# The opening of a two-layer graph transformer kernel, written out by hand: biases placed by matmuls, W1 split on VectorE, scores of group 1 ahead of the first PV, W2 loaded in two parts

## The chip, the cores and the metric

The kernel runs on one core of one Trainium2 chip. The metric is the device time in microseconds (us), lower is better. Below, TensorE is PE in the rows, VectorE is DVE, ScalarE is ACT, GpSimd is POOL and SyncE, which issues the DMAs, is SP.

## The reference

Input x is 128 graphs of 64 nodes with 384 features, adj is 128 x 64 x 64. Everything is fp32. Two layers follow each other.

```python
# layer 0: 8 heads of 48, feed-forward 384 -> 1536 -> 384
q, k, v = x @ wq + bq, x @ wk + bk, x @ wv + bv
attn = softmax(q @ k.T * 48**-0.5 + adj)
x1 = alpha1 * rms(x + (attn @ v) @ wo + bo) + gamma1
z  = alpha2 * rms(x1 + silu(x1 @ w1 + b1) @ w2 + b2) + gamma2
x  = layernorm(x + z)
# layer 1: 12 heads of 32, weights transposed, adj added twice (spatial and edge)
x  = layernorm(x + attention(x, 2 * adj) @ Wo.T + bo)
```

## The kernel before, in words

The 8192 nodes are cut into 32 groups of 256 (two tiles of 128, each of two graphs). Layer 0 goes through all groups, then layer 1; this case is about the opening of layer 0. Every fp32 matrix product is made of three passes over a high and a low part (`mm3`, L421): each operand is rounded on ACT ("high") and the rest is formed on DVE by a subtraction ("low"). So each weight and each activation is converted once on ACT and once on DVE before TensorE can read it.

Layer 0 is a software pipeline over steps g. In step g TensorE does, in this written order, `pv` of group g-1 (probabilities times v), `scores` of g, the feed-forward of g-2 (`ffn1` and `ffn2` in six blocks, with `attn_out` of g-1 in its middle), and `qk` and `values` of g+1. In the steps 0 to 2 `qk` and `values` of g+1 stand ahead of the feed-forward instead (`ahead`). Each engine has its own list in program order and waits on semaphores; nothing reorders at run time. SP's list is the only one that issues DMAs, so a load that waits holds back every load and store behind it.

Between the matrix products there are three round trips through DRAM, which turn a tile of rows into a tile of columns: DVE transposes 32x32 blocks, SP stores them in eight DMAs, waits for them, and loads the turned tile in one DMA; ACT and DVE make its high and low part. The round trips are p (`turn_p` L873, `store_p` L245, `load_pt` L252, `take_pt` L650), the context (`turn_ctx` L889, `store_ctx` L261, `load_ctxt` L265, `ctxt_high` L658), and x1 (`turn_x1` L912, `store_x1` L269, `load_x1t` L273, `x1t_high` L664, `turned_low` L832). Buffers are shared: the turned p lands in the buffer from which the next `add_adj` (L852) writes, so this waits until `take_pt` has copied it; the context's and x1's transposes both write `blocks`, so `turn_ctx` of group 1 waits until x1 of group 0 is stored, and `turn_x1` until the context is stored. `swap_v` (L238) copies halves of the v tiles within SBUF by four DMAs a group, after `keep_v` (L632).

The opening also loads and splits the weights. wk comes in three pieces, wq, wv and wo in one each, W1 in three thirds of 512 columns, W2 in twelve pieces of 128 rows; all stand in work buffers that are free then. `high` (L596) and `low` (L801) split the first four, `w1_high` on ACT and `w1_low` (L1081) on GpSimd W1, `w2_high` and `w2_low` W2. The biases of q and k have to be put in the order in which the heads lie in the partitions: SP writes them to DRAM by single elements (L324) and, when that is done, reads them back by columns (L334). The first feed-forward waits for the whole of W1 (`ffn1`, L514), for all of W2 (L540, and ACT at L673) and for x1 of group 0. W2's second half is loaded, split and waited for at the end of step 1, behind x1's load. x of group 2 and 3 (`load_xt`) is issued behind the load of the turned p.

## Time and profile before

| what | us |
|---|---|
| median of 3 runs (1997.39 to 2000.54) | 1998.48 |
| the profiled execution | 1995.27 |
| its span | 1993.5 |
| TensorE busy in the span | 1909.8 (96%) |
| DVE / ACT / GpSimd busy | 1259.4 / 1059.1 / 413.6 |

Busy time of TensorE is that of overlapping matmuls and says nothing of its peak. The rows below give times from the start of the span; the first number of a chain or timeline row is the start, the second the length. A loop pass of layer 0 is the step g from 4 on.

### The profile page before, as it was taken

What the parts mean: (1) busy time and instruction counts of PE and PEld (TensorE: products, weight loads), DVE (VectorE), ACT (ScalarE), POOL (GpSimd) and SP (SyncE); (2) the same over time, 40 slices, a digit from 0 to 9 for tenths busy, and PEclk for the clock granted to TensorE, in tenths of its full rate; (3) what the DMA queues carried; (4) which work ended last, traced back from release to release, by engine and by line L of the source; (5) the groups of instructions that cost most, each with busy time, mean ns of one, the idle gap of its engine ahead of it and who ended that gap; (6) DMA issues with size and microseconds to landing.
All of it is one profiled execution on the core that took longest, in us unless ns stands there. A gap on an engine that the chain in (4) does not pass through costs nothing.

```text
span 1993.5 us, 55130 instructions
## 1 busy us (share of the span) xinstructions
PE 1909.8 (96%) x20800; PEld 1879.3 (94%) x20800; DVE 1259.4 (63%) x2469; ACT 1059.1 (53%) x2270; POOL 413.6 (21%) x555
## 2 busy tenths in 40 slices
PE   5499999999999999999999999999799999999997
PEld 5489999999999999999999999988799999999997
DVE  3546666666656666666666666655566676666775
ACT  3346554565555655556555565444355555555555
POOL 1202211312113121121212212121122222222222
PEclk9699999999999999999999999999899999999999
DMA  7534444444454444444344443444222222222222
GB/s 170 147 84 118 119 112 131 110 123 117 105 137 106 121 116 114 129 108 125 109 122 120 111 126 106 126 107 104 77 76 85 87 79 78 79 83 87 87 79 66
DMA packets 269817, 213.61 MB, mean 107 GB/s; under 512 B 143952, under 2 KB 252240, under 8 KB 269776
## 3 DMA queue, kind: packets, MB, share of 16 engines
q1 hardware_dynamic: 269776, 213.05, 39.3%
q8 instruction: 27, 0.44, 0.1%
q14 instruction: 14, 0.11, 0.0%
HBM read 120.34 MB, written 79.69 MB: 100 GB/s over the span
## 4 chain that ended last, share of the span: by engine, by line
PE 91%; DVE 3%; DMA 2%; SPq 1%; ACT 1%; issue 1%; POOL 0%; ACTq 0%; POOLq 0%; DVEq 0%
PE a_bank L424 31%; PE a_banks L424 29%; PE b_bank L1276 15%; PE b_banks L1276 5%; PE b_bank L1343 2%; PE a_bank L473 2%; PE b_banks L1330 2%; PE a_banks L493 2%; PE b_banks L1320 2%; PE b_bank L1353 1%; SPq L258 1%; DMA a_hid_stage<-in_L_gnn_w 1%; DMA a_work<-x_turned 1%; DMA a_work<-in_L_gnn_wk 1%; DMA x_turned<-a_work 0%
## 5 line engine op out<-in xcount | busy, mean ns | idle before, releaser
L424 PE MATMUL a_bank<-a_x1t_hi,a_w_hi 128*128 128x256 f32 x1152 | 330.1, 287 | 13.8 <-DVE a_x1t_lo L834 12.2
L424 PE MATMUL a_bank<-a_x1t_hi,a_w_lo 128*128 128x256 f32 x1152 | 326.6, 284 | 0.0
L424 PE MATMUL a_bank<-a_x1t_lo,a_w_hi 128*128 128x256 f32 x1152 | 326.5, 283 | 0.0
L679 ACT ACTIVATE a_work<-a_bank,a_b 128x256 f32<-128x256 f32 x384 | 160.0, 468 | 218.4 <-PE a_bank L424 218.0
L424 PE MATMUL a_banks<-a_w_hi,a_hid_hi 128*128 128x384 f32 x768 | 259.7, 338 | 0.1
L424 PE MATMUL a_banks<-a_w_hi,a_hid_lo 128*128 128x384 f32 x768 | 259.4, 338 | 0.0
L424 PE MATMUL a_banks<-a_w_lo,a_hid_hi 128*128 128x384 f32 x768 | 259.2, 338 | 0.0
L849 DVE TENSOR_TENSOR a_hid_lo<-a_work,a_hid_hi 128x512 fp32r<-128x512 f32 x192 | 131.3, 697 | 195.4 <-ACT a_hid_hi L684 195.4
L424 PEld LDWEIGHTS a_bank<-a_x1t_hi,a_w_hi 128*128 128x128 f32 x1152 | 219.2, 190 | 16.6 <-DVE a_x1t_lo L834 12.9
L424 PEld LDWEIGHTS a_bank<-a_x1t_lo,a_w_hi 128*128 128x128 f32 x1152 | 219.5, 191 | 0.0
L424 PEld LDWEIGHTS a_bank<-a_x1t_hi,a_w_lo 128*128 128x128 f32 x1152 | 219.5, 191 | 0.0
L1104 POOL TENSOR_TENSOR a_ms<-a_ssq,eps_rms 128x2 f32<-128x2 f32 x64 | 12.6, 196 | 659.3 <-ACT a_work L689 659.3
L424 PEld LDWEIGHTS a_banks<-a_w_hi,a_hid_hi 128*128 128x128 f32 x768 | 144.3, 188 | 0.3 <-DVE a_hid_lo L849 0.3
L424 PEld LDWEIGHTS a_banks<-a_w_hi,a_hid_lo 128*128 128x128 f32 x768 | 144.5, 188 | 0.0
L424 PEld LDWEIGHTS a_banks<-a_w_lo,a_hid_hi 128*128 128x128 f32 x768 | 144.2, 188 | 0.0
L667 ACT ACTIVATE a_x1t_hi<-a_work 128x768 fp32r<-128x768 f32 x32 | 27.1, 846 | 211.7 <-DMA a_work<-x_turned 211.7
L684 ACT ACTIVATE a_hid_hi<-a_work 128x512 fp32r<-128x512 f32 x192 | 121.5, 633 | 8.4
L424 PE MATMUL a_bank<-xt_hi,wk_hi 128*128 128x256 f32 x288 | 84.9, 295 | 35.5 <-DVE xt_lo L820 19.8
L1619 POOL TENSOR_TENSOR b_p<-b_score,b_smax 128x768 f32<-128x768 f32 x64 | 93.1, 1476 | 114.8 <-DVE b_smax L1530 114.8
L843 DVE TENSOR_TENSOR a_work<-a_banks,a_bv 128x384 f32<-128x384 f32 x64 | 35.7, 558 | 111.2 <-PE a_banks L424 111.2
L1512 DVE TENSOR_TENSOR b_v_nat<-b_bank,bv_l 128x384 f32<-128x384 f32 x64 | 35.6, 557 | 101.3 <-PE b_bank L1276 101.3
L1427 ACT ACTIVATE b_p<-b_p 128x768 f32<-128x768 f32 x64 | 54.1, 847 | 81.1 <-POOL b_p L1619 81.1
(166 smaller groups left out, 5506.3 us busy)
## 6 DMA issues: line engine op xcount, KB each, us to landing
a_work<-in_x SPq DMA_DIRECT2D x64, 384.0 KB, 3.2
p_turned<-a_work SPq DMA_DIRECT2D x256, 64.0 KB, 2.2
a_work<-p_turned SPq DMA_DIRECT2D x32, 512.0 KB, 3.2
xt_raw<-in_xT SPq DMA_DIRECT2D x32, 384.0 KB, 3.8
ctx_turned<-a_work SPq DMA_DIRECT2D x256, 48.0 KB, 1.7
a_work<-ctx_turned SPq DMA_DIRECT2D x32, 384.0 KB, 3.2
x_turned<-a_work SPq DMA_DIRECT2D x256, 48.0 KB, 1.7
a_work<-x_turned SPq DMA_DIRECT2D x32, 384.0 KB, 3.8
```

The costliest lines, as they stand in the source:

```text
L424: r = pe.matmul(out, lhs[a], rhs[b], start=first and n == 0, stop=last and n == 2)
L473: r = pe.matmul(PV_BANK[t][64 * s:64 * s + 64, h * 2 * VW:(h + 1) * 2 * VW].rearrange("p (r c) -> p r c", r=2), pt[:, t, s * 256 + h * 64: ...
L493: r = pe.matmul(s_banks[64 * s:64 * s + 64, i, at:at + n * NODES].rearrange("p (e n) -> p e n", e=n), q[row, m, nodes], k_t[row, m:m + n, ...
L679: r = act.activation(silu[:, p % 2, s * GROUP:(s + 1) * GROUP], A[p % 3][:, s * GROUP:(s + 1) * GROUP], ACT.Silu, bias=b1[:, m:m + 1])
L684: act.activation(hid[0][:, p % RING, :], silu[:, p % 2, :], ACT.Copy).then_inc(hid_hi, 1)
L849: dve.tensor_tensor(hid[1][:, p % RING, :], silu[:, p % 2, :], hid[0][:, p % RING, :].bitcast(F32), ALU.subtract).then_inc(hid_lo, 1)
L1276: r = pe.matmul(out, lhs[a], rhs[b], start=first and n == 0, stop=last and n == 2)
L1320: r = pe.matmul(four[64 * s:64 * s + 64, i, at:at + NODES], qk_t[row, k, nodes], qk_t[row, KT + k, nodes], start=True, stop=True, skip_gro ...
L1330: r = pe.transpose(two[t][:, h * P:(h + 1) * P], prob[:, t, h * P:(h + 1) * P], ident[:])
L1343: r = pe.matmul(one[PV_BANK[t]][64 * s:64 * s + 64, h * 2 * VW:(h + 1) * 2 * VW].rearrange("p (r c) -> p r c", r=2), pt[:, t, h * P + 64 * ...
L1427: act.activation(prob[:, t, :], prob[:, t, :], ACT.Exp, scale=2.0).then_inc(exp_done, 1)
L1619: pool.tensor_tensor(p, s, smax[:, t, :].unsqueeze(2).broadcast_to([P, H1, NODES]), ALU.subtract).then_inc(shifted, 1)
```

## The change

All of it is in the opening of layer 0, which becomes one list per engine (`begin()`), up to and including the first feed-forward. The loop from step 3 on is as it was.

- Biases: bq and bk are loaded as they are (128 x 3). Two matmuls with the identity turn them into rows, DVE spreads and sorts them (in p's and pt's buffers, then unused), six matmuls of one column each put them into the partitions, and DVE reads them from PSUM. TensorE has the first two ahead of its first `qk`, the six behind it.
- W1: its low parts are made on DVE, one third in each of three places; the slots are three different buffers (no third waits for another), and TensorE and ACT wait for a third or for all at their own places.
- Order on TensorE: scores of group 1 come ahead of PV of group 0; `attn_out` of group 0 comes ahead of PV of group 1 and is behind `qk` and `values` of group 2; scores of group 2 and `qk`, `values` of group 3 follow, and then the first feed-forward.
- W2: twelve buffers instead of six; the first six pieces are issued behind xt of group 3, the other six behind the load of x1 of group 0, and they are split on ACT and DVE inside the first feed-forward, whose blocks wait for two pieces each.
- SP: x of group 1 is issued ahead of the v swaps of group 2, which stand ahead of x1's store; xt of group 2 stands behind the v swaps of group 0, ahead of p's store; W1's second third behind it, its last third behind the load of p.

The core of the diff (removed lines first where they differ; waits on constants and slots left out):

```diff
@@ SBUF slots
-w1_slots = [work[:, start[n]:start[n] + KT * 512].rearrange("p (k c) -> p k c", k=KT) for n in ("x1", "x_bo")]
+w1_slots = [work[:, start[n]:start[n] + KT * 512].rearrange("p (k c) -> p k c", k=KT) for n in ("x1", "spare")]
 w1_slots.append(hid_stage[0][:])
 w2_slots = [work[:, start["silu"] + i * D:start["silu"] + (i + 1) * D] for i in range(2)]
 w2_slots += [hid_stage[1][:].rearrange("p r c -> p (r c)")[:, i * D:(i + 1) * D] for i in range(4)]
+w2_slots += [work[:, start[n] + i * D:start[n] + (i + 1) * D] for n, k in (("spare", 4), ("x_res", 2)) for i in range(k)]
+spread = v["p"][0:KT, 0:2 * D].rearrange("p (b d) -> p b d", b=2)
+sorted_rows = v["pt"][0:KT, 0:2 * D].rearrange("p (b m c) -> p b m c", b=2, m=KT)
...
@@ sync: loads
...
     def load_w2(which):
         for i in which:
-            if i >= len(w2_slots):
-                sp.wait_ge(w2_lo, i - len(w2_slots) + 1)
-            sp.dma_start(w2_slots[i % len(w2_slots)], w["w2"][i * P:(i + 1) * P, :]).then_inc(
-                w2_loaded[i % len(w2_slots)], 16)
+            sp.dma_start(w2_slots[i], w["w2"][i * P:(i + 1) * P, :]).then_inc(w2_loaded[i // 2], 16)
...
-    load_piece(sp, pieces[0], w_loaded[0], by_block=False)
-    for name in ("bq", "bk"):
-        sp.dma_start(scratch[name].rearrange("(k p) -> p k", p=P), w[name],
-                     allow_slow_non_contiguous=True).then_inc(bias_placed, 16)
-    for i in range(1, WQ + 1):
-        load_piece(sp, pieces[i], w_loaded[i], by_block=False)
-    sp.dma_start(shared["ident"][:], w["ident"]).then_inc(early_loaded, 16)
-    sp.wait_ge(bias_placed, 32)
-    for dst, name in ((bq, "bq"), (bk, "bk")):
-        pairs = scratch[name].rearrange("(i y) -> i y", y=2 * DH0)
-        each = scratch[name].rearrange("(h y) -> h y", y=DH0)
-        for m, part in enumerate((pairs[:, 0:WHOLE], pairs[:, DH0:DH0 + WHOLE], each[:, WHOLE:DH0])):
-            sp.dma_start(dst[:, m:m + 1], part).then_inc(early_loaded, 16)
...
+    def begin():
+        load_xt(0)
+        for i in range(WK + 1):
+            load_piece(sp, pieces[i], w_loaded[i], by_block=False)
+        for dst, name in ((bq_raw, "bq"), (bk_raw, "bk"), (shared["ident"], "ident")):
+            sp.dma_start(dst[:], w[name]).then_inc(bias_loaded, 16)
+        for i in (WQ, WV):
+            load_piece(sp, pieces[i], w_loaded[i], by_block=False)
+        load_row(bv, "bv", early_loaded)
+        load_row(rows["bo"], "bo", early_loaded)
+        load_adj(0)
+        load_xt(1)
+        load_piece(sp, pieces[WO], w_loaded[WO], by_block=True)
+        load_w1(0)
+        sp.wait_ge(pairs_zeroed, 1)
+        sp.wait_ge(ones_set, 1)
+        for t in range(TILES):
+            swap_v(0, t)
+        load_xt(2)
+        load_adj(1)
+        sp.wait_ge(w_lo, WV + 1)
+        load_w1(1)
+        for t in range(TILES):
+            store_p(0, t)
+        load_pt(0)
+        load_w1(2)
+        load_x(0)
+        load_consts()
+        for t in range(TILES):
+            swap_v(1, t)
+        for t in range(TILES):
+            store_ctx(0, t)
+        load_adj(2)
+        load_ctxt(0)
+        for t in range(TILES):
+            store_p(1, t)
+        load_pt(1)
+        load_xt(3)
+        load_w2(range(0, 6))
+        load_x(1)
+        for t in range(TILES):
+            swap_v(2, t)
+        for t in range(TILES):
+            store_x1(0, t)
+        load_x1t(0)
+        sp.wait_ge(w1_lo, 2)
+        load_w2(range(6, FC))
+        for t in range(TILES):
+            store_ctx(1, t)
+        load_adj(3)
+        load_ctxt(1)
+        for t in range(TILES):
+            store_p(2, t)
+        load_pt(2)
+        load_late()
+        load_x(2)
+        for t in range(TILES):
+            store_x1(1, t)
+        load_x1t(1)
+        sp.wait_ge(w2_lo, FC)
+        load_res(0)
...
@@ tensor
     def ffn1(f, p, new, back):
         if p == 0:
-            if isinstance(f, int) and f == 0:
-                pe.wait_ge(w1_lo, N_W1)
             pe.wait_ge(x1t_lo, f + 1)
+        if isinstance(f, int) and f == 0 and p % 2 == 0:
...
-            if isinstance(f, int) and f == 0:
-                pe.wait_ge(w2_lo, FC)
+        if isinstance(f, int) and f == 0:
+            pe.wait_ge(w2_lo, 2 * p + 2)
...
+    def bias_rows():
+        pe.wait_ge(bias_loaded, 16 * N_BIAS)
+        for j, raw in enumerate((bq_raw, bk_raw)):
+            r = pe.matmul(PV_BANK[0][0:KT, j * P:(j + 1) * P], raw[:], shared["ident"][:], start=True, stop=True,
+                          skip_group_check=True)
+        r.then_inc(bias_row, 1)
+    def place_bias():
+        pe.wait_ge(bias_sorted, 1)
+        pe.wait_ge(one_set, 1)
+        for j in range(2):
+            for m in range(KT):
+                at = 2 * P + j * KT + m
+                r = pe.matmul(PV_BANK[0][:, at:at + 1], sorted_rows[:, j, m, :], one_row[0:KT, :], start=True, stop=True,
+                              skip_group_check=True)
+        r.then_inc(bias_placed, 1)
+    def begin():
+        bias_rows()
+        qk(0)
+        place_bias()
+        for t in range(TILES):
+            values(0, t)
+        scores(0)
+        qkv(1)
+        scores(1)
+        for t in range(TILES):
+            pv(0, t, True)
+        qkv(2)
+        for t in range(TILES):
+            attn_out(0, t, True)
+        for t in range(TILES):
+            pv(1, t, True)
+        scores(2)
+        qkv(3)
+        feed_forward(0, True, True)
...
@@ scalar
         if isinstance(f, int) and f == 0 and p == 0:
-            act.wait_ge(w2_lo, FC)
+            act.wait_ge(w2_lo, 6)
+            act.wait_ge(w1_lo, N_W1)
...
+    def begin():
...
+        for t in range(TILES):
+            keep_v(0, t)
+        for t in range(TILES):
+            exp(0, t)
+        high(pieces[WO], w_loaded[WO], 64, w_hi)
+        for u in (1, 2):
+            take_q(1, u)
+        split_x(2)
+        w1_high(0)
+        for t in range(TILES):
+            take_pt(0, t)
+        for t in range(TILES):
+            keep_v(1, t)
+        w1_high(1)
+        for t in range(TILES):
+            exp(1, t)
+        for u in (1, 2):
+            take_q(2, u)
+        w1_high(2)
+        ctxt_high(0)
+        split_x(3)
+        for t in range(TILES):
+            square(x1, y1_done, ssq1, sq1_done, t + 1, t, ctxt[:, t, :])
+        for t in range(TILES):
+            take_pt(1, t)
+        w2_high(range(0, 6))
+        for t in range(TILES):
+            keep_v(2, t)
+        for t in range(TILES):
+            exp(2, t)
+        for u in (1, 2):
+            take_q(3, u)
+        x1t_high(0)
+        act.wait_ge(const_loaded, 16 * N_CONST)
+        for p in range(2):
+            hidden(0, p)
+        w2_high(range(6, FC))
+        ctxt_high(1)
+        for p in (2, 3):
+            hidden(0, p)
+        for t in range(TILES):
+            square(x1, y1_done, ssq1, sq1_done, TILES + t + 1, t, ctxt[:, t, :])
+        for p in (4, 5):
+            hidden(0, p)
+        for t in range(TILES):
+            take_pt(2, t)
+        x1t_high(1)
+        mean_square(0)
...
@@ vector
+    def spread_bias():
+        dve.wait_ge(bias_row, 1)
+        dve.tensor_tensor(spread.rearrange("p b (k c) -> p b k c", k=KT),
+                          PV_BANK[0][0:KT, 0:2 * P].rearrange("p (b c) -> p b c", b=2).unsqueeze(2).broadcast_to([KT, 2, KT, P]),
+                          shared["ident"][0:KT, 0:KT].unsqueeze(1).unsqueeze(3).broadcast_to([KT, 2, KT, P]),
+                          ALU.mult).then_inc(bias_spread, 1)
+    def sort_bias():
+        dve.wait_ge(bias_spread, 1)
+        for m in range(KT):
+            r = dve.tensor_copy(by_head(sorted_rows.rearrange("p b m c -> p b (m c)"), m, False), by_head(spread, m, True))
+        r.then_inc(bias_sorted, 1)
+    def take_bias():
+        dve.wait_ge(bias_placed, 1)
+        at = 2 * P
+        dve.tensor_copy(bk[:], PV_BANK[0][:, at + KT:at + 2 * KT])
+        dve.tensor_scalar(bq[:], PV_BANK[0][:, at:at + KT], SCALE0, None, ALU.mult).then_inc(bias_set, 1)
...
+    def begin():
+        dve.memset(one_row[:], 1.0).then_inc(one_set, 1)
+        split_x(0)
+        for i in range(WK + 1):
+            low(pieces[i], w_hi, i + 1, w_lo)
+        spread_bias()
+        low(pieces[WQ], w_hi, WQ + 1, w_lo)
+        sort_bias()
+        dve.tensor_reduce(mask[:], shared["ident"][:].rearrange("p (i e c) -> p e i c", e=2, c=PART),
+                          mybir.AxisListType.XY, ALU.add).then_inc(mask_set, 1)
+        low(pieces[WV], w_hi, WV + 1, w_lo)
...
+        take_bias()
...
+        take_k(0)
+        for t in range(TILES):
+            take_v(0, t)
+        split_x(1)
+        for t in range(TILES):
+            add_adj(0, t)
+        for t in range(TILES):
+            shift(0, t)
+        for t in range(TILES):
+            turn_p(0, t)
+        take_k(1)
+        low(pieces[WO], w_hi, WO + 1, w_lo)
+        for t in range(TILES):
+            take_v(1, t)
+        split_x(2)
+        w1_low(0)
+        for t in range(TILES):
+            add_adj(1, t)
+        for t in range(TILES):
+            take_ctx(0, t)
+        for t in range(TILES):
+            turn_ctx(0, t)
+        for t in range(TILES):
+            shift(1, t)
+        for t in range(TILES):
+            turn_p(1, t)
+        w1_low(1)
+        take_k(2)
+        for t in range(TILES):
+            take_v(2, t)
+        turned_low(ctx_t, turned_raw, ctxt_hi, ctxt_lo, 1)
+        split_x(3)
+        w1_low(2)
+        for t in range(TILES):
+            take_y1(0, t)
+        dve.wait_ge(const_loaded, 16 * N_CONST)
+        scale_x1(0)
+        for t in range(TILES):
+            turn_x1(0, t)
+        for t in range(TILES):
+            take_ctx(1, t)
+        for t in range(TILES):
+            add_adj(2, t)
+        for t in range(TILES):
+            turn_ctx(1, t)
+        for t in range(TILES):
+            shift(2, t)
+        w2_low(range(0, 6))
+        for t in range(TILES):
+            turn_p(2, t)
+        take_k(3)
+        for t in range(TILES):
+            take_v(3, t)
+        turned_low(x1_t, x1t_raw(0), x1t_hi, x1t_lo, 1)
+        for p in range(2):
+            hidden_low(0, p)
+        w2_low(range(6, FC))
+        turned_low(ctx_t, turned_raw, ctxt_hi, ctxt_lo, 2)
+        for p in (2, 3):
+            hidden_low(0, p)
+        for t in range(TILES):
+            take_y1(1, t)
+        hidden_low(0, 4)
+        scale_x1(1)
+        for t in range(TILES):
+            turn_x1(1, t)
+        hidden_low(0, 5)
+        for t in range(TILES):
+            take_y2(0, t)
+        turned_low(x1_t, x1t_raw(1), x1t_hi, x1t_lo, 2)
...
@@ gpsimd
-    for i in range(N_W1):
-        w1_low(i)
...
+    def begin():
+        bias_x(0)
+        root(0, ssq1, sq1_done, ms1, ms1_done, eps_rms, rstd1, rstd1_done)
+        pool.wait_ge(const_loaded, 16 * N_CONST)
+        add_b2(0)
+        bias_x(1)
+        root(1, ssq1, sq1_done, ms1, ms1_done, eps_rms, rstd1, rstd1_done)
+        root2(0)
+        add_b2(1)
```

## Rows read from the trace of the kernel before

**Rows 1.** Busy time by stretches: stretch, then busy us (count) by engine, PEclk, DMA, GB/s.
```profile
0.00:154.30 154.30, 101.62 (x1039) 98.40 (x1039) 73.79 (x132) 60.27 (x134) 28.81 (x29) 0.85 0.52 132
...
200.00:1300.00 1100.00, 1100.00 (x10529) 1088.60 (x10527) 708.63 (x1386) 604.76 (x1359) 222.12 (x316) 1.00 0.44 118
```
**Rows 2.** TensorE's longest wait in the first 160 us: total, times, longest.
```profile
PE a_bank L424 <- DVE xt_lo L820: 19.8, 2, 14.2
```
**Rows 3.** The chain in order of time: start, length, what.
```profile
3.13 10.34 DMA a_work<-in_L_gnn_wk
...
15.68 8.54 PE a_bank L424 x54
...
28.09 1.47 PE a_banks L493 x75
...
111.06 6.64 PE a_bank L424 x54
...
144.93 0.96 DVE a_x1t_lo L834
```
**Rows 4.** DMA issues to 160 us: KB each, median us to landing.
```profile
a_work<-in_L_gnn_w SPq DMA_DIRECT2D x12, 192.0 KB, 7.2
...
bk_by_row<-in_L_gnn_bk SPq DMA_DIRECT2D x1, 1.5 KB, 9.7
```
**Rows 5.** SP's timeline: store of p, its load, context store, its load, x1 store.
```profile
34.16 4.55 SPq L249 DMA_DIRECT2D p_turned<-a_work x8
40.16 0.34 SPq L254 DMA_DIRECT2D a_work<-p_turned x1
...
57.29 3.65 SPq L258 DMA_DIRECT2D ctx_turned<-a_work x8
...
62.84 0.34 SPq L267 DMA_DIRECT2D a_work<-ctx_turned x1
...
83.14 3.65 SPq L258 DMA_DIRECT2D x_turned<-a_work x8
```
**Rows 6.** ACT's timeline: first wk piece, copy of p, v tile, two W2 pieces.
```profile
5.18 0.69 ACT L600 ACTIVATE wk_hi<-a_work 128x128 fp32r<-128x128 f32 x3
...
44.00 1.33 ACT L654 ACTIVATE a_work<-a_work 128x256 f32<-128x256 f32 x4 [4.46 <-DMA a_work<-p_turned]
...
51.69 0.35 ACT L637 ACTIVATE a_work<-a_work 64x196 f32<-64x196 f32 x1
...
62.19 0.92 ACT L612 ACTIVATE a_w_hi<-a_work 128x384 fp32r<-128x384 f32 x2
```
**Rows 7.** DVE's timeline, second round.
```profile
51.81 3.55 DVE L820 TENSOR_TENSOR xt_lo<-xt_raw,xt_hi 128x768 fp32r<-128x768 f32 x1 [11.87 <-ACT xt_hi L617]
55.28 0.19 DVE L881 RECIPROCAL a_rden<-a_bank 128x8 f32<-128x8 f32 x1
...
56.69 1.03 DVE L893 STREAM_TRANSPOSE a_work<-a_work 128x384 f32<-128x384 f32 x2
57.64 1.25 DVE L859 TENSOR_TENSOR a_work<-a_banks,a_adj 128x512 f32<-128x512 f32 x2
58.81 0.67 DVE L868 TENSOR_REDUCE a_smax<-a_work 128x8 f32<-128x512 f32 x1
...
61.44 0.70 DVE L875 STREAM_TRANSPOSE a_work<-a_work 128x512 f32<-128x512 f32 x1
...
68.16 1.02 DVE L815 TENSOR_TENSOR a_w_lo<-a_work,a_w_hi 128x384 fp32r<-128x384 f32 x2
...
78.09 0.56 DVE L901 TENSOR_TENSOR a_work<-a_banks,a_work 128x384 f32<-128x384 f32 x1 [2.27 <-PE a_banks L424]
```
**Rows 8.** GpSimd's timeline: the last third of W1.
```profile
51.12 3.42 POOL L1083 TENSOR_TENSOR a_w_lo<-a_hid_stage,a_w_hi 128x1536 fp32r<-128x1536 f32 x1 [6.87 <-ACT a_w_hi L607]
```
**Rows 9.** DVE by form, first 154 us: busy us, mean ns.
```profile
L828 DVE TENSOR_SCALAR a_work<-a_bank,a_bk,a_mask 128x256 f32<-128x256 f32 x8 | 3.9, 533 | 0.0
...
L809 DVE TENSOR_TENSOR wo_lo<-a_work,wo_hi 128x1152 fp32r<-128x1152 f32 x1 | 1.3, 1345 | 0.0
```

More of the change, by code:

```diff
@@ L406, in _ @@
+            begin()
             step(3)
@@ L725, in step @@
                         keep_v(g, t)
-                if ffn and not ahead:
+                if ffn:
                     hidden(f, 0)
@@ L730, in step @@
                         exp(g, t)
-                if first:
-                    high(pieces[WO], w_loaded[WO], 64, w_hi)
-                    for i in range(2):
-                        w1_high(i)
-                if second:
-                    w2_high(range(0, 6))
-                if ahead:
-                    for u in (1, 2):
-                        take_q(g + 1, u)
-                if ffn and ahead:
-                    x1t_high(f)
-                    hidden(f, 0)
                 if ffn:
                     hidden(f, 1)
-                if nxt and not ahead:
+                if nxt:
                     split_x(g + 1)
@@ L773, in step @@
                         take_pt(g, t)
-                if first:
-                    w1_high(2)
-                if second:
-                    w2_high(range(6, FC))
-                if back and not second:
+                if back:
                     x1t_high(b)
-                if nxt and not ahead:
+                if nxt:
                     for u in (1, 2):
@@ L978, in next_x, with step @@
                                   ALU.subtract).then_inc(shared["next_xt_lo"], 1)
-            def step(g, new=True, nxt=True, back=True, ffn=True, late=True):
+            def step(g, new=True, nxt=True, back=True, ffn=True):
                 b, f, e = g - 1, g - 2, g - 3
-                first, second = new and not back, back and not ffn
-                ahead = nxt and isinstance(g, int) and g < 3
-                if ahead and not first:
-                    split_x(g + 1)
                 if back:
@@ L995, in step @@
                         shift(g, t)
-                if ffn and not ahead:
+                if ffn:
                     hidden_low(f, 0)
@@ L1044, in step @@
                     dve.wait_ge(late_loaded, 16 * N_LATE)
-                if late:
-                    layer_norm(e, g + 1 if new else NG)
-                if nxt and not ahead:
+                layer_norm(e, g + 1 if new else NG)
+                if nxt:
                     take_k(g + 1)
@@ L1051, in step @@
                         take_y2(f, t)
-                if back and not second:
+                if back:
                     turned_low(x1_t, x1t_raw(b), x1t_hi, x1t_lo, b + 1)
-                if second:
-                    w2_low(range(6, FC))
-                if nxt and not ahead:
+                if nxt:
                     for t in range(TILES):
```

233 lines of the change are left out of this document (73 added, 160 removed).

## The prediction

> **What bounds the kernel now.** I read three views in this order. The table by stretches says where TensorE is short of work: from 200 to 1300 us it is busy for 1100 of 1100 us at a granted clock of 1.00, while in the first 154.3 us it is busy for 101.6 us only, at a mean clock of 0.85 [rows 1]. So 52.7 us of idle time, and some half-speed time beside it, lie in the opening, and nothing lies in the loop that follows. Everything the diff touches is in the opening; whatever time it moves the first loop pass by, the end moves by, as long as the loop stays full. The list of waits then names the largest single cause: input tiles (xt_lo) for 19.8 us in two waits, the longest 14.2 [rows 2]. The chain in order of time gives the anchors that I shift below: TensorE starts at 15.68 us because the last pieces of wk come 10.34 us after their issue; the first scores start at 28.09; the first feed-forward starts at 111.06; the second x1 is split at 144.93 + 0.96, and the loop is full from then on [rows 3].
>
> The rule of my sum is therefore: new start of the first feed-forward, against 111.06, then see whether anything between it and 144.93 becomes longer.
>
> **Start: biases.** Removed are two loads of 384 four-byte elements, which took 9.7 us to land (the second) [rows 4] and stood ahead of the last pieces of wk, and six column loads behind a wait of SP. Added are three loads (two of 128 x 12 bytes, one of 64 KB that was there before), two small fp32 matmuls ahead of the first QK, six tiny ones behind it, and on DVE one multiply over 768 columns, three copies and two PSUM reads. The first wk piece, issued at 1.24, is at ACT at 5.18 [rows 6], 3.9 us later. The third piece is now issued at about 2.2 and is ready at 6.5 (some bandwidth added), high and low part 0.7 each: 8. The bias loads are issued at 2.7 to 4.2 and land at 8.1; two matmuls, an estimate of 1 us; TensorE starts QK at about 9.5, with 0.4 of reserve. From both sides: not before 8 (wk itself), and not after about 12.4, if 256 small packets hold the queue as the 768 did, a third of 10.34 us or 3.4. The trace shows no such packets of 12 bytes; I take the value near the lower end, since there are a third as many and each is three times as large. From TensorE's start to the first scores it was 28.09 - 15.68 = 12.4 us [rows 3], all of it matmuls and one v tile, and placing the biases adds an estimated 1.0 (between 0.3, six matmuls of 50 ns, and 2): first scores at 22.9 instead of 28.09. DVE's bias work lies beside QK's first matmuls; if that cover were gone it would cost 2 us.
>
> The Trainium skill, "DMA: Bandwidth & Descriptors", section Specifications, wants at least 512 bytes a transfer for full rate. The trace agrees for the four-byte loads. The rule would put the new 12-byte loads in the same class, which is my upper bound of 12.4 for the start and 3 us less gain; it changes the range, not the likeliest case.
>
> **First probabilities.** From the scores' start to the first store of p it was 34.16 - 28.09 = 6.1 us [rows 3, 5], now 29.0. SP has ten issues ahead of it that used to stand behind or elsewhere (four v swaps from about 24.2, xt of group 2, adj, four of W1's second third); eight issues take 4.55 us [rows 5], so SP is there at 29.5 or so. Store to load is 40.16 - 34.16 = 6.0, load to ACT's first use 44.00 - 40.16 = 3.8 [rows 5, 6], and I add 0.5 for W1's traffic ahead: p is back at 39.8 instead of 44.0. Meanwhile TensorE does QK and V of group 1 and now its scores too, ahead of the first PV, to about 36.5: these scores fill time in which it stood. What they cannot do is start softmax 1 at once: adding adj to group 1 waits until p 0 is copied out of the shared buffer.
>
> **Second round, from 39.8.** Copy p 1.33 [rows 6] to 41.1. Add adj 57.64 to 58.81, 1.2; context and its transposes 55.28 to 57.64, 2.4 [rows 7]: first transpose ready 44.2, all at 44.7. Store context to its load is 62.84 - 57.29 = 5.55 [rows 5]: 49.8. Store of p 1 is queued behind that load on SP, from 50.2 (its data is ready at 44.7 + 2.6 + 1.5 = 48.8 by rows 7, so SP's order decides); 6.0 to its load, 56.2; xt of group 3 is issued behind it at 56.6 and lands at 61.0 (3.8 as above and 0.4 MB more). ACT and DVE split it, 1.8, 62.8. Then the new place of W1: its last third is split on DVE behind xt, 1536 columns at 1.345 us for 1152 [rows 9], 1.8 each; 64.6. Only now come the two additions y1 of group 0, to 65.7; the second begins at 65.2 (before: 78.09 [rows 7]). The attention output itself is done earlier, by 61.6 even at half clock, so it is covered by 3 us.
>
> **x1 and the queues that it is moved past.** From the second y1 to the store of x1 it was 83.14 - 78.09 = 5.05 [rows 5, 7]: 70.2. But SP first issues x of group 1, which waits for y1, and then the v swaps of group 2. These wait for ACT: squares 0.7, copy of p 1 1.3 (so PV 1 starts at 67, TensorE idle from 59 or so), six W2 pieces at 0.46 [rows 6], two v tiles at 4 x 0.36 [rows 6]: 71.9. Four swaps at half of 4.55 end at 73.6. x1's store starts there, 3.4 late, and takes 5.5 to complete: 79.1. DVE has context 1 ready long before, but its transpose writes the buffer that x1's store reads, so DVE stands until 79.1, and behind it are queued: two transposes 1.0, softmax 2 58.81 to 61.44 2.6, six W2 pieces from 68.16 2.8, two transposes of p 1.4 [rows 7], k 1.4 from three operations of about 0.5 [rows 9], v 1.1, and the split of x1 0.96 [rows 3]. Sum 11.3: the first feed-forward starts at 90.4. x1 itself is loaded by 83 and waits for DVE there. 111.06 - 90.4 = 20.6 us gained.
>
> **W1 off GpSimd.** Before, the last third took 3.42 us there from 51.12 [rows 8], and in that time DVE's split of xt, 0.96 us undisturbed, took 3.55 us from 51.81 [rows 7]. Now DVE does three pieces in 5.4 us. The first two lie in time in which DVE waits for p or SP does; the third is in the chain, counted above. If the second lost its cover that is 1.8 more.
>
> The Trainium skill, "SBUF — State Buffer", section SBUF: two separate sides, calls the port pair of DVE and GpSimd an exclusive lock: an operation with two SBUF inputs is blocked for the whole of a GpSimd one. The trace agrees: 51.12 + 3.42 is 54.5, and the split ends at 55.4, its own length later. The rule also speaks against the change: the two additions of bo to x 0 (about 2.7 us) now fall on softmax 1 near 44 to 47 us. By it p 1 is ready at up to 50.9 instead of 48.8 and the gain is 20 us; without it 20.6.
>
> **Inside the first feed-forward.** It was 34.8 us from its start to the second x1's split [rows 3]. W2's second half moves into it: on ACT 2.8 and on DVE 2.8 us between its second and third block. TensorE wants context 1 about 13 us after the start, DVE delivers it at 10.5; with 2.4 us of cover I count 0 (if W2 comes late it costs one for one; issued at 79.5 it is due at 87 by the 7.2 us of rows 4, and wanted at 96). The loads of p 2, the late rows and x 2 have reserves of over 8 us.
>
> Sum: the profiled execution took 1995.27 us (span 1993.5), so 1974.7; the median shown, 1998.48, is 3.2 above that execution, so I forecast 1978 us, on its own 1973 to 1984.
>
> **Rivals.**
> (a) Traffic crowds the chain. W1's second third is issued just ahead of p 0's store, W2's first half right behind xt 3, W1's last third and the rows just ahead of context 0. A W piece took 7.2 us in the middle [rows 4] against 3.8 for a load in quiet; if p 0 and xt 3 each pay that difference of 3.4 us, the gain is 14: 1985 us. For it: both lie in stretches with several MB queued. Against: the loads named are mostly queued behind, not ahead.
> (b) Transfers are quicker, and SP's queue thinner, than the old rows: x1's store goes out at 70.2 as soon as turned (3.4 us), and the start is at 8 (1.5): gain 25.5, 1973 us. For it: the 10.34 us are a trait of the removed loads alone. Against: the keeping of v 2 stands behind W2 on ACT by the written order.
> (c) Slower: the loop does not close up. If the other phase in which DVE, ACT and SP enter it left TensorE waiting once a pass, 28 passes at 1 us are 28 us against 20.6 won: 2006 us. It decides from 0.75 us a pass. Against it: after the old opening the loop has no idle time at all from 200 us on [rows 1], and TensorE's own work in a pass fills it whatever the start.
> (d) The opening is as long as before, because the same ring of stores and loads (p, context, x1) sets it: 1998. Against: the ring is 45 us from p 0 to x1's split here, and was 67 (44.0 to 111.06).
>
> **How the numbers follow.** Forecast 0.56, (a) 0.20, (b) 0.18, (c) 0.04, (d) 0.02. 0.2% of the time is 4 us, about what a measurement of this kernel tells from no change. Faster by more 0.93 (the first three less a little for a very crowded (a)), within 0.03, slower 0.04. The range reaches from (b) with its landings 3 us quicker still, 1970, to (a) with 3 us more for a late start, 1988.
>
> **What would show it.** First QK matmul near 9.5 and no 10 us wait on wk; first scores near 23; p 0 at ACT near 40; a DVE gap of some 5 us before the context-1 transpose that ends with x1's store; first feed-forward near 90; no idle TensorE from 135 us on. Wrong would be: TensorE idle beyond 150 us, a W1 or W2 wait inside the first feed-forward, or an x1 store that SP starts before the swaps of v 2.

## The result, and the profile after

The changed kernel takes 1966.01 us (median of 4 runs, 1965.19 to 1970.78), beside 1998.47 for the kernel before on the same chip: ratio 0.984, 95% interval 0.982 to 0.986, 32.5 us less. I had forecast 1978, 20.5 less, on its own 1973 to 1984. So the sign held, and so did the mechanism of the opening; the size did not: 12 us of the gain are in no step of my sum. The profiled execution took 1970.78 us (span 1968.9), the longest of the four; so the difference of the two profiled executions, 24.6 us of span, understates the gain.

The stretches that answer to [rows 1], in the kernel after:
```profile
0.00:154.30 154.30, 118.12 (x1172) 114.19 (x1173) 88.91 (x164) 71.85 (x160) 19.09 (x30) 0.90 0.53 145
200.00:1300.00 1100.00, 1098.93 (x10719) 1086.75 (x10718) 712.86 (x1397) 608.58 (x1371) 228.85 (x324) 1.00 0.44 119
```
In the opening TensorE is busy for 118.1 instead of 101.6 us and its mean granted clock is 0.90 instead of 0.85. The second line holds a hint of what I had ruled out. TensorE is busy all the time in both kernels, yet it did 10719 matmuls in the 1100 us instead of 10529. Not all of this is speed: a window cuts the passes at another place when the opening is shorter, and the matmuls are of very different sizes. The first experiment below, which has the new opening and passes as long as before, counts 10642. What shows a faster loop is the length of a pass.

Its chain of waits in order of time (start, length, what), which answers to [rows 3] and gives the steps of the sum:
```profile
8.16 8.52 PE a_bank L441 x54
...
35.59 6.35 DMA a_work<-p_turned
41.95 0.73 ACT a_work L703 x2
...
59.57 4.64 DMA xt_raw<-in_xT
...
65.98 1.75 DVE a_w_lo L893
...
77.14 0.59 SPq L262
...
80.62 1.67 DMA x_turned<-a_work
...
93.19 8.47 PE a_bank L441 x54
...
127.44 0.96 DVE a_x1t_lo L912
...
177.55 3.51 DMA ctx_turned<-a_work
181.07 3.50 DMA a_work<-ctx_turned
```
The 10.34 us on wk are gone, TensorE starts at 8.16, the first feed-forward at 93.19 instead of 111.06, and the second x1 is split at 127.44 instead of 144.93: 17.5 us earlier. The last two lines are a context round trip in which both transfers were slow, 7.0 us; TensorE stood for it, and the first pass of the loop took 44.89 us (159.07 to 203.96) instead of 40.84. In the kernel below that has the same opening in the old places, TensorE is busy for all of 150 to 200 us (50.00 of 50), so I take these 4 us for an accident of the profiled execution, and not for a trait of the change. Another wait for a context, 1.1 us at the end of the loop near 1291, is no such accident: the profiles of all kernels with the new opening have it (0.4 to 1.4 us).

DVE's timeline: the addition of adj to group 1, that to group 2, and the gap that I had named; the bracket is the idle time before the instruction and what ended it:
```profile
43.42 1.29 DVE L937 TENSOR_TENSOR a_work<-a_banks,a_adj 128x512 f32<-128x512 f32 x2 [5.89 <-ACT a_work L703]
...
74.88 1.28 DVE L937 TENSOR_TENSOR a_work<-a_banks,a_adj 128x512 f32<-128x512 f32 x2
82.39 1.04 DVE L971 STREAM_TRANSPOSE a_work<-a_work 128x384 f32<-128x384 f32 x2 [6.24 <-DMA x_turned<-a_work]
```
TensorE's waits in the first 160 us: total, times, longest, which answer to [rows 2]:
```profile
PE a_bank L490 <- ACT a_work L703: 13.6, 2, 7.1
PE a_bank L441 <- DVE a_x1t_lo L912: 10.7, 2, 8.8
```
The 19.8 us on xt are gone; what is late next is p's round trip and the first x1.

Where the loop's time comes from is seen when one pass of each kernel's chain is laid beside the other. The kernel before, one pass from 1180.54 to 1221.84, 41.30 us:
```profile
1180.54 6.61 PE a_bank L424 x54
...
1189.26 2.13 PE a_bank L424 x18
...
1203.00 6.34 PE a_banks L424 x36
1209.34 6.48 PE a_bank L424 x54
...
1221.84 6.61 PE a_bank L424 x54
```
The kernel after, 1196.78 to 1237.62, 40.84 us:
```profile
1196.78 6.34 PE a_bank L441 x54
...
1205.20 2.12 PE a_bank L441 x18
...
1218.88 6.25 PE a_banks L441 x36
1225.12 6.48 PE a_bank L441 x54
...
1237.62 6.34 PE a_bank L441 x54
```
The order and the numbers of matmuls are the same. The first line of each is half of a group's `ffn1`, 54 products that read x1: 6.34 instead of 6.61 us, 117 instead of 122 ns each. The line x36 is `ffn2`, reading the hidden activations: 6.25 instead of 6.34. QK of the next group (the second x54), which reads xt, is as it was: 6.48. The line x18 is one of three blocks that make up the other half of `ffn1`; they read x1 and W1 too, and have hardly changed: 2.13 and 2.12. In the kernel before, the starts of the first and the last of the loop's 28 QK blocks lie 1115.10 us apart, 27 passes of 41.30; 27 x 0.46 = 12 us. The list of these instructions was not changed, but something that they use was: bq_raw, bk_raw and one_row, allocated ahead of them (and bq_scaled gone), moved the context, x1 and hidden tensors by 64 bytes within a partition. W1, W2 and xt lie below and did not move.

### The profile page after: what moved, and what is told of

Its sections match the earlier page's. It is cut to its first block, busy times and chain, and to the rows that moved or that the text cites. A ratio compares the mean times of both kernels' runs of the same rounds, so it can differ in the third digit from the quotient of the medians.

```text
span 1968.9 us, 55169 instructions
## 1 busy us (share of the span) xinstructions
PE 1899.2 (96%) x20816; PEld 1867.3 (95%) x20816; DVE 1261.6 (64%) x2478; ACT 1056.1 (54%) x2270; POOL 402.3 (20%) x552
## 4 chain that ended last, share of the span: by engine, by line
PE 90%; DMA 3%; DVE 3%; SPq 3%; ACT 1%; issue 1%; POOL 0%; ACTq 0%; POOLq 0%; DVEq 0%
PE a_bank L441 29%; PE a_banks L441 28%; PE b_bank L1423 16%; PE b_banks L1423 5%; PE b_bank L1490 2%; PE a_bank L490 2%; PE b_banks L1477 2%; PE b_banks L1467 2%; PE a_banks L510 2%; SPq L262 1%; PE b_bank L1500 1%; DMA a_work<-x_turned 1%; DMA ctx_turned<-a_work 0%; DMA xt_raw<-in_xT 0%; DMA x_turned<-a_work 0%
## 5 line engine op out<-in xcount | busy, mean ns | idle before, releaser
L1423 PE MATMUL b_bank<-xt_hi,wq_hi 128*128 128x256 f32 x288 | 88.3, 306 | 2.8 <-DVE xt_lo L1644 2.8
```

Source lines behind the costliest of these rows:

```text
L1423: r = pe.matmul(out, lhs[a], rhs[b], start=first and n == 0, stop=last and n == 2)
```

## The experiments

Each was timed beside the kernel before on its own chip; that kernel's median was 1997.1 to 1999.6 us in all of them. The kernels were timed on several chips, so a difference between the times of two changed kernels is known to some 2.5 us only, unless their profiles confirm it. Theory L said that these 64 bytes are the loop's gain, its rival that it is the other phase in which the engines enter the loop, or the place of the loop's instructions.

**The kernel after in the old places.** The edit moves the three new tensors behind all others, and 12 bytes keep the place of bq_scaled:
```diff
+        pad = sb("a_pad", [P, KT])
-        bq_raw, bk_raw, one_row = ...      # now the last tensors of the layer
```


> The changed kernel with its three new small tensors moved to the end of the layer's buffers and 32 bytes of padding in the place of the one it removed, so that the work buffer, the turned context and x1 and the hidden blocks lie at the byte addresses of the kernel before (64 bytes lower than in the changed kernel). Nothing else differs. Theory L (layout): the 0.455 us by which a loop pass became shorter (41.30 to 40.85, 26 passes, 11.8 us) come from the 64 bytes by which these buffers moved; expected pass 41.30 us, time 1966 + 12 = 1978. Theory C (code): they come from where the loop's instructions lie or from how the opening hands over; expected pass 40.85, time 1966.

Measured: 1977.63 us (1975.86 to 1979.97), ratio 0.990 [0.988, 0.991]. Chain, in the loop:
```profile
1202.50 6.61 PE a_bank L442 x54
...
1224.96 6.34 PE a_banks L442 x36
```
All old lengths are back (QK is 6.48 here too), the pass is 41.30, and the first and last QK block lie 1115.10 us apart as in the kernel before. This is the opening alone: 21.9 us, on 20.5 forecast. In its profiled execution the second x1 is split at 125.61, 19.3 us before [rows 3], and the span is 1974.3, 19.2 shorter. So "the end moves by what the opening moves" holds, once the addresses are held.

**The kernel before, moved by 64 bytes.** The other half of the same test:
```diff
+        pad = sb("a_pad", [P, 16])         # ahead of the layer's work tensors
```


> The kernel before with 64 bytes of padding ahead of its work buffer, nothing else. Theory L: pass 40.85 us instead of 41.30 and 12 us less, 1986.5, with the opening as it was. Theory C: pass 41.30, 1998.5.

Measured: 1981.62 (1980.99 to 1982.95), ratio 0.991 [0.990, 0.993]. The chain, a pass of 40.83 us:
```profile
1192.28 6.25 PE a_banks L425 x36
1198.53 6.48 PE a_bank L425 x54
...
1211.03 6.34 PE a_bank L425 x54
```
With the old opening, hence the old phase, and with no instruction changed, the loop has the new speed. The kernel before had a median of 1999.5 on this chip, so 17.9 us were gained, on 12 expected. The two profiled executions are 13.8 us of span apart (1993.5 and 1979.7), of which the loop's 27 passes are 12.5 (1115.10 to 1102.62). The other 4 us are between executions that were not profiled: the profiled one of the kernel before took 1995.27, 4.2 under the median of 1999.5.

**Only x1 moved, in the kernel before:**
```diff
         ctx_t = ...
+        pad0 = sb("a_pad0", [P, 16])
         x1_t = ...
+        pad1 = sb("a_pad1", [P, 48])       # everything behind lies 256 bytes on
```


> The kernel before with 64 bytes of padding ahead of the turned x1 alone, and 192 behind it (so what follows lies 256 bytes on). By theory L, if it is the moving operand of the first feed-forward product that is read faster from its new address: matmuls that read x1 every 116.5 ns instead of 119.7, 108 x 3 of them less 3 ns, so a pass of 40.97; the products that read the hidden blocks stay at 175.8 ns. If the work buffer's address matters instead (what the other engines write and read meanwhile), 41.30 remains.

Measured: 1986.59 in one execution; the chain, a pass of 41.03 (1172.64 to 1213.67), 40.98 in the mean of 27, on 40.97 expected:
```profile
1194.83 6.34 PE a_banks L426 x36
...
1213.67 6.34 PE a_bank L426 x54
```
The block of 54 with x1 is fast, the block of 36 with the hidden tensor as slow as before: each changes with the place of its own operand. This is not the whole story. The block of 30 products of the context and of hidden activations, none of which was moved modulo 256 bytes, takes 5.29 or 5.34 us here instead of 5.23; no run shows why.

**Is it the address, or the distance to the weights?** Three placements of the kernel after: 64 bytes more, 32 bytes more, and 64 bytes ahead of everything (weights and all):
```diff
+        pad = sb("a_pad", [P, 16])         # "shift_more64"; [P, 8] in "shift_more32"; behind one_row
+        pad_front = sb("pad_front", [P, 16])   # "front_shift64": the first tensor of all
```


> The changed kernel with 64 bytes more ahead of the work buffer: the turned x1 lies at 224 modulo 256 (96 in the kernel before, 160 in the changed one). If the address modulo 128 sets the rate of the products of the feed-forward, a loop pass is 41.30 us again; if 64-byte steps matter modulo 256, it is neither of the two; if only the old address was bad, it stays at 40.85.

> The changed kernel with 32 bytes more ahead of the work buffer: x1 at 192 modulo 256, 64 modulo 128, a multiple of 64. If multiples of 64 are read best, the pass is below 40.85; if the address modulo 128 matters in a step between 32 and 96, it is 40.85 or 41.30.

> The changed kernel with 64 bytes ahead of all buffers, the weights too: each product's two operands keep their distance, while all of them move by 64. If the distance of weights and moving operand counts, the pass stays at 40.85 us; if the address itself counts, it changes, and the layer-1 pass (17.65 us) may change as well, since its weights and inputs move too.

Measured, one execution each: 1980.66, 1981.53 and 1962.58 us, with passes of 41.31, 41.32 and 40.81. The chains of the three in this order:
```profile
1204.88 6.67 PE a_bank L442 x54
...
1225.29 2.15 PE a_bank L442 x18
...
1227.44 6.25 PE a_banks L442 x36
```
```profile
1187.20 6.36 PE a_banks L442 x36
...
1206.06 6.59 PE a_bank L442 x54
```
```profile
1191.82 6.32 PE a_bank L441 x54
...
1213.88 6.25 PE a_banks L441 x36
```
In the first and the third, x1 starts at the same byte, 206048 of a partition, 64 above its place in the kernel after, yet the block takes 6.67 in one and 6.32 in the other. So it isn't the address of x1 alone; where x1 lies against W1 fits all four placements, and a pass of layer 1, whose operands all moved by 64 bytes in the third kernel, stays at 17.66. In the second, x1 starts at a multiple of 64 bytes, and the pass is not below 40.85: an aligned start is not what counts. All placements of this study, as the distance of the activation's high part from the weight's, modulo 256 bytes, from the addresses in the built programs (low parts stand at the same distances):

| products of | distance | block of the chain, us | in |
|---|---|---|---|
| x1 with W1, x54 | 128 | 6.61 | before, old places |
| | 192 | 6.34 (6.32) | after, before moved, x1 alone, front |
| | 224 | 6.59 | 32 more |
| | 0 | 6.67 | 64 more |
| x1 with W1, x18 | 128 / 192 / 224 / 0 | 2.13 / 2.12 / 2.13 / 2.15 | before / after / 32 more / 64 more |
| hidden with W2, x36 | 128 / 224 | 6.34 / 6.36 | before, x1 alone / 32 more |
| | 192 / 0 | 6.25 / 6.25 | after, front / 64 more |
| xt with wq and wk, x54 | 96 | 6.48 | all but the last kernel below |

Two things keep this table from being a law. The blocks of 18 are products of the same two tensors at the same distances, and they take 118 to 119 ns a matmul throughout, while the block of 54 goes from 122 to 117 (its first matmul takes over 220 ns in both; behind it the starts lie 118.7 and 113.6 ns apart in the timelines). Something besides the distance decides how much it is worth: the blocks differ in what stands around them, in the columns of W1 and in their PSUM bank, and no run separates these. And in the x36 rows the roles are exchanged: in `ffn1` and QK the weight is the stationary operand (128x128) and the activation the moving one (128x256), in `ffn2` the hidden activation is stationary and W2 moves (128x384). Counted as moving less stationary, the hidden rows stand at 128 and 32 (slow) and at 64 and 0 (fast), so they can't be compared number by number with those of x1.

**The v swaps of group 2 behind x1's store.** My sum priced the x1 store as 3.4 us late behind four swaps.
```diff
-                for t in range(TILES):
-                    swap_v(2, t)
                 for t in range(TILES):
                     store_x1(0, t)
                 load_x1t(0)
+                for t in range(TILES):
+                    swap_v(2, t)
```


> The changed kernel with SP's list altered in one place: x1 of group 0 is stored and loaded ahead of the v swaps of group 2. Theory Q (SP's order holds x1 back, as the prediction has it): the store starts at 73.6 instead of 77.1 and DVE's stand before the context transpose ends 3.5 us earlier, so the first feed-forward starts near 89.7 instead of 93.2 and the time is 3.5 us less, 1962.5. Rival: the swaps, now 5 us later, hold v of group 3 on DVE (it waits for them) or PV of group 2, and the gain is below 1.5 us, or a loss.

Measured: 1962.16 us (1960.7 to 1962.54), ratio 0.982 [0.980, 0.983], 3.9 less than after. The chain:
```profile
74.71 1.68 DMA x_turned<-a_work
...
76.48 1.04 DVE a_work L971 x2
...
87.28 8.13 PE a_bank L441 x54
```
The store is done 5.9 us earlier, DVE's gap shrinks from 6.2 to 2.8, and the feed-forward starts 5.9 earlier. Of this, 2.4 is a quicker xt 3 in this execution (ready at 61.8 instead of 64.2) and 3.5 the swaps; between medians it is 3.9 (two chips), beside the 3.4 of my sum.

**W1's low parts back on GpSimd** (`w1_low(0..2)` at the head of GpSimd's list, out of DVE's three places):
```diff
-                w1_low(0)                  # DVE; likewise w1_low(1), w1_low(2)
+                for i in range(N_W1):      # GpSimd, ahead of bias_x(0)
+                    w1_low(i)
```


> The changed kernel with W1's low parts back on GpSimd (ahead of its other work), all else as changed. Theory Q (the chain as the prediction has it): the last third leaves DVE's list ahead of y1 (1.75 us less there), but GpSimd's thirds of 3.4 us now meet DVE's operations with two SBUF inputs (softmax 1 at 47 to 50 us, the split of context 0 at 57.6) and cost 1 to 2 there: 0 to +1.5 us against the changed kernel, 1966 to 1967.5. Rival: moving W1 to DVE is a main part of the gain; then 4 us or more are lost, 1970.

Measured: 1964.42 (1960.32 to 1965.91), ratio 0.982 [0.980, 0.983], 1.6 less than after, within the spread of both. The first feed-forward starts at 91.37, 1.8 earlier, about the length of the split in the chain. So the expected 0 to 1.5 us of loss did not come, nor the rival's 4: W1 on DVE is no part of the gain.

**The written order of TensorE: PV of group 0 ahead of scores of group 1:**
```diff
-                scores(1)
                 for t in range(TILES):
                     pv(0, t, True)
+                scores(1)
```


> The changed kernel with TensorE's order of before at one place: PV of group 0 ahead of the scores of group 1. Theory Q: the scores no longer fill the time in which p 0 is away, so they end some 2.2 us after PV (at half clock), and DVE, which adds adj to group 1 before it takes context 0, starts at about 47.8 instead of 43.4; everything behind is 4 us later: 1970. Rival: other queues cover it and less than 1 us is lost, 1966.5.

Measured: 1967.07 (1966.81 to 1972.08), ratio 0.985 [0.983, 0.986]; the chain:
```profile
40.90 2.88 PE a_bank L490 x32
43.78 1.84 PE a_banks L510 x76
```
and DVE's addition of adj to group 1:
```profile
45.64 1.29 DVE L937 TENSOR_TENSOR a_work<-a_banks,a_adj 128x512 f32<-128x512 f32 x2 [6.99 <-PE a_banks L510]
```
Between medians 1.1 us are lost, within what can be told from nothing, so the time alone speaks for the rival. The profile speaks for theory Q: the addition now waits for the scores on TensorE and starts 5.5 us after p is at ACT (40.12), while in the kernel after it waits for ACT's copy of p and starts 1.5 us after that (41.95 to 43.42). The order costs 4 us at this place; p came back 1.8 us earlier (its load took 3.37 us here), and the first feed-forward starts at 94.47, 1.3 later than after. How much of the 4 us reaches the end stays open.

**The biases by way of DRAM again**, in the new opening (the two loads by single elements behind wk's first piece, six column loads, neither matmuls nor DVE's sorting):
```diff
-                for dst, name in ((bq_raw, "bq"), (bk_raw, "bk"), (shared["ident"], "ident")):
-                    sp.dma_start(dst[:], w[name]).then_inc(bias_loaded, 16)
+                for name in ("bq", "bk"):
+                    sp.dma_start(scratch[name].rearrange("(k p) -> p k", p=P), w[name], ...)
```


> The changed kernel with the biases of q and k placed through DRAM as before, all else as changed. Theory Q: the first scores are at about 28.1 again instead of 22.2, SP's list is free before p 0 is turned, and the whole of the 5.9 us is lost: 1972. Rival: p 0's return is held by the loads around it (it took 6.35 us here against 3.84), which then have drained, and only 3 us are lost: 1969.

Measured: 1971.35 (1970.78 to 1972.1), ratio 0.986 [0.984, 0.987]; the chain:
```profile
3.13 12.66 DMA a_work<-in_L_gnn_wk
...
18.00 8.41 PE a_bank L449 x54
```
TensorE starts 9.8 us later. p is at ACT 6.8 later (48.77), since its load took 3.63 us instead of 6.35, as the rival had it; the first feed-forward starts 7.5 later (100.64), and the medians are 5.3 apart, near the 6 of theory Q. So the start is worth some 5 of the opening's 22 us.

**x of group 3 converted behind W2** (`split_x(3)` behind `w2_high` and `w2_low` of the last six, on ACT and DVE):
```diff
                 ctxt_high(0)
-                split_x(3)
...
+                x1t_high(0)
+                w2_high(range(6, FC))
+                split_x(3)
                 for u in (1, 2):
                     take_q(3, u)
```


> The changed kernel with the order of before at one place: ACT and DVE split W2's second half ahead of xt of group 3 (its load is where it was), so that QK and V of group 3 come right ahead of the first feed-forward. Theory W (most of what the opening won is that QK and V of group 3 no longer stand behind W2's second half): y1 no longer waits for xt 3 and everything up to x1's load is 7 us earlier, W2 is there at about 82 instead of 89, then xt's split, QK and V, 12 us on TensorE alone, and the first feed-forward starts at 98.5 instead of 93.2: 1971. Rival Q (the gain is in the shorter round trips, and W2's place costs nothing of its own): what y1 gains makes up for it, within 2 us of 1966.

Measured: 1972.97 (1969.98 to 1973.76), ratio 0.987 [0.986, 0.989], 7 us worse than after, on 5 expected by theory W. TensorE's longest wait:
```profile
PE a_bank L441 <- DVE xt_lo L898: 21.2, 1, 21.2
```
y1 comes 5 us earlier, at 62.7, but QK of group 3, ahead of the feed-forward in TensorE's list, now waits, and the feed-forward starts at 102.57 (theory W: 98.5). The place where xt 3 stands in the change is the better one.

**The best version: x1's store first, and all three pairs at 192.** It is the store edit above with pads that put xt at 192 from wq and wk, and the context of both layers at 192 from wo; x1 and hidden keep the distance that they have in the kernel after:
```diff
+        pad_xt = sb("pad_xt", [P, 24])     # ahead of xt
+        pad0 = sb("a_pad0", [P, 16])       # ahead of the context
+        pad1 = sb("a_pad1", [P, 48])       # behind it
+        pad0 = sb("b_pad0", [P, 56])       # layer 1, ahead of its context
```


> A candidate: the changed kernel with x1's store ahead of the v swaps (1962.2 in the earlier run), and padding such that the two operands of every three-part product lie 192 bytes apart modulo 256: xt and the attention weights (96 so far), the contexts of both layers and wo (32 and 128 so far); x1 and W1, the hidden blocks and W2 have this distance already. Theory D (the distance sets the rate; where it was 192 the first 54 products of the feed-forward took 6.34 us, at 0, 128 or 224 they took 6.60 to 6.67): QK's 54 products, now 6.48 us, go to 6.34 in each of the 64 passes, 0.14 us each, 9 us, and the output products a little: 1953. Rival: QK's rate is its own and only the blocks right behind the scores react; then 1962.

Measured: 1947.86 us (1946.4 to 1949.48), ratio 0.975 [0.974, 0.977], beside 1997.11 for the kernel before on this chip; 18 us under after and 5 under the expectation. The chain:
```profile
1203.60 6.25 PE a_banks L443 x36
1209.85 6.14 PE a_bank L443 x54
...
1222.01 6.34 PE a_bank L443 x54
```
xt's block goes from 6.48 to 6.14, the pass to 40.5; a pass of layer 1, of which the expectation had only its QK, goes from 17.65 to 17.44 us. 27 x 0.33 + 32 x 0.21 = 15.6. Measured against the kernel with the store edit alone it is 14.3 between medians, but these were taken on two chips: each against its own before it is 11.9 (49.3 and 37.3), and the two profiled executions are 12.5 us of span apart. Here the distance was chosen beforehand for pairs that had never been moved, and the time followed.

## Why the prediction was wrong

The step that failed stands in its first paragraph: "nothing lies in the loop that follows. Everything the diff touches is in the opening; whatever time it moves the first loop pass by, the end moves by". I took a TensorE that is busy all the time at full clock for one that can't be faster. What the runs showed in its place: the diff did touch the loop, since its three small tensors move the operands of the loop's matmuls by 64 bytes, and a pass takes 40.84 instead of 41.30 us. Between medians 21.9 us are the opening (the old places against before) and 11.6 the pass (the old places against after, 1977.63 - 1966.01); the measured 32.5 is within a microsecond of their sum. Rival (c), a loop of another length, had the right place but only one sign; I gave a faster loop no chance.

The steps of the opening, as forecast, and as in the kernel after:

- Biases: start at 9.5, measured 8.16. The two loads of 12-byte rows, issued behind the wk pieces, landed in 3.1 and 2.9 us:
```profile
a_bq_raw<-in_L_gnn_bq SPq DMA_DIRECT2D x1, 1.5 KB, 3.1
a_bk_raw<-in_L_gnn_bk SPq DMA_DIRECT2D x1, 1.5 KB, 2.9
```
The upper bound of 12.4 did not come. The Trainium skill, "DMA: Bandwidth & Descriptors", section Specifications, wants at least 512 bytes a transfer for full rate; a wk piece of 192 KB landed in 3.6 us beside them, so these landings show no cost of it. That the removed loads cost the 10 us is shown by putting them back (12.66). First scores: 22.9, measured 22.17.
- First probabilities: p's store at 29.5, measured 30.26; p at ACT at 39.8, measured 41.95, because its load took 6.35 us in this execution. With the store edit it was back 3 us earlier, and with PV first at 40.12: the load took 3.4 to 6.6 us in the profiles of kernels whose lists are the same up to it, more than my error.
- Second round: xt 3 ready for ACT at 61.0, measured 64.23, of which 2.2 is inherited from p, 0.8 was lost between p and the issue of the load (59.57), and 0.2 is its length, 4.64. W1's third split in the chain: 1.8, measured 1.75. That adding adj waits for the copy of p, as the sum had it, is so: it started 1.5 us behind p at ACT. With PV first it would have started 5.5 behind; the sum gave this order no price.
- Port lock. The addition of bo ran on GpSimd from 46.29 for 1.99 us:
```profile
46.29 1.99 POOL L1231 TENSOR_TENSOR a_work<-a_work,a_bo 128x384 f32<-128x384 f32 x2 [43.92 <-DMA a_work<-in_x]
```
DVE's subtraction of two SBUF inputs at 48.01 took 0.82 us instead of the 0.69 of its twin at 49.46, 0.13 more and not up to 2: the two hardly met, since DVE was transposing and reducing, with one input, from 46.4 to 48. This agrees with the lock of the Trainium skill, "SBUF — State Buffer", section SBUF: two separate sides, which names DVE operations with two SBUF inputs.
- x1: the store behind the swaps at 73.6, measured 77.14. The swaps began at 73.72 instead of 71.9, 1.8 late, and the four took 3.4 us. I had meant half of 4.55 and added 1.7 only (71.9 + 2.3 is 74.2), so 0.6 of the error is a slip of the sum. Its mechanism is as forecast: DVE's gap was to end at 79.1 and ended at 82.39, and the swaps' share, 3.4 us, was 3.5 between the profiles and 3.9 between medians.
- First feed-forward: 90.4, measured 93.19 (91.21 in the kernel in the old places). From there to x1's split 34.8, measured 35.2 (127.44 + 0.96 - 93.19): W2's second half is hidden, as costed.

So the opening's working was right in sum: 1974.7 for the profiled execution, against 1976.11 in the old places, where p is at ACT at 40.58, xt 3 is ready at 62.52 and the first feed-forward starts at 91.21. In the profiled execution of the kernel after its steps were up to 3.5 us late. Rival (a), crowded traffic, had some of its price (p and xt 3, 3 us in the profiled execution) and not its 6.8. Rival (b) was right on the start, 8.16, and wrong in its chief part: x1's store did not go out as soon as it was turned. Rival (c) did not come: the passes have no repeated wait. Rival (d) is refuted; the ring that I put at 45 us against it is 50.6 by my own steps (39.8 to 90.4) and was 51.2.

What stays open: why the distance counts, and why for the blocks of 54 and hardly for those of 18; whether 256 bytes is the period (for x1 alone, 64 modulo 128 would fit the four distances as well; the hidden products, slow at 128 and fast at 0, speak against that); the 30-product block of the kernel with x1 alone moved; and some 4 us of the moved kernel before.

## What to carry to other kernels

A stretch in which the bounding engine is 100% busy can still become faster or slower: compare the length of its passes and blocks before and after, not only its idle time. A count of instructions in equal windows misleads when the phase has moved: here it rose by 113 of 10529 with no change in speed. A change that allocates even a few bytes moves every tensor behind them; to know what an edit of the schedule is worth, hold the addresses with a pad, and time the pad alone as well. Where a loop is bound by matmuls from SBUF, trying a few offsets between operands is cheap: here it brought 12 to 14 us in 1962, with no instruction changed.

## What the runs showed of the hardware that I had not expected

- At a granted clock of 1.00, the 54 matmuls (128 x 256, high and low parts) that open the feed-forward take 6.34 us with the two SBUF operands 192 bytes apart modulo 256, and 6.59 to 6.67 at 0, 128 and 224; those of xt 6.14 at 192 and 6.48 at 96. That is 114 to 117 against 120 to 124 ns each. The same pair moved together by 64 bytes keeps its speed (6.32). Blocks of 18 of the same products take 2.12 to 2.15 at all four distances.
- Two loads of 384 single elements hold the wk pieces behind them to 10.34 and 12.66 us; two of 128 rows of 12 bytes, issued behind all wk pieces, land in 3.1 and 2.9 us and delay nothing that the trace shows. How much of this is the order and how much the size of the elements was not separated.
